# A copy moved from ScalarE to GpSimd, and channel factors moved from SBUF to PSUM, in a kernel of four line scans and a dynamic-kernel convolution block

## The reference, cut to what matters

```python
def step(prev, cur):
    new = cur + jax.nn.relu(_row_conv(prev, K))     # 9 taps, 64 -> 64 channels
    return (new, new)
```

```python
pooled = x.mean((2, 3)); hdn = _ln(pooled @ w_fc1.T, ln1_w, ln1_b); dyn = hdn @ w_fc2.T
out = depthwise_conv(x, dyn.reshape(b * c, 1, 5, 5), pad=2)
out = layer norm of out over the channels
out = gelu(einsum('bchw,oc->bohw', out, w_expand))            # 64 -> 256 channels
gx = sqrt(sum(out ** 2, axis=(2, 3)));  nx = gx / (gx.mean(1) + EPS)
out = g * (out * nx) + bt + out                                # the "response"
return einsum('bohw,co->bchw', out, w_shrink) + x
```

## Time and profile before

| | us |
|---|---|
| median of 3 runs | 860.77 (859.72 to 861.04) |
| profiled execution, its own time | 859.75 |
| its span | 857.8 |
| TensorE busy in the span | 783.1 (91%) |
| VectorE busy | 620.9 (72%) |
| GpSimd busy | 454.5 (53%) |
| ScalarE busy | 407.9 (48%) |

### The profile page before, as it was taken

How to read it: one execution, slowest core, us unless ns; L and a number is a source line. 1 busy time by engine, 2 the same in 40 slices (tenths; PEclk the granted TensorE clock), 3 DMA queues, 4 the chain that set the end, 5 groups by cost and what they waited for, 6 DMA issues and landing times. The chain is left out here.

```text
span 857.8 us, 15635 instructions
## 1 busy us (share of the span) xinstructions
PE 783.1 (91%) x5399; PEld 637.1 (74%) x5399; DVE 620.9 (72%) x1130; ACT 407.9 (48%) x495; POOL 454.5 (53%) x444
## 2 busy tenths in 40 slices
PE   5999999999999999999999957677899998999796
PEld 5999998999999999999999956444444444444232
DVE  4666666666666666658888867888889898998944
ACT  5690004767770000000000014389999999999771
POOL 2333333333333333338888845698686787877520
PEclk9999999999999999999999978799999999999999
DMA  6760000000000000000000010221234343333314
GB/s 145 166 157 0 0 0 2 0 0 0 0 1 1 0 0 0 0 1 1 0 0 0 0 49 0 64 64 51 55 93 100 87 99 76 77 79 86 84 34 99
DMA packets 61572, 35.81 MB, mean 42 GB/s; under 512 B 41504, under 2 KB 59488, under 8 KB 61536
## 3 DMA queue, kind: packets, MB, share of 16 engines
q1 hardware_dynamic: 61536, 35.36, 17.2%
HBM read 17.85 MB, written 9.37 MB: 32 GB/s over the span
## 5 line engine op out<-in xcount | busy, mean ns | idle before, releaser
L481 PE MATMUL psum<-line_hi,taps_hi 128*128 128x256 f32 x1270 | 203.0, 292 | 11.7 <-DVE taps_lo L377 8.4
L495 PE MATMUL psum<-line_lo,taps_hi 128*128 128x256 f32 x1270 | 202.5, 291 | 0.9 <-DVE line_lo L430 0.8
L489 PE MATMUL psum<-line_hi,taps_lo 128*128 128x256 f32 x1270 | 202.3, 291 | 0.0
L430 DVE SCALAR_TENSOR_TENSOR line_lo<-psum,rest 128x256 fp32r<-128x256 f32 x254 | 108.1, 426 | 123.9 <-POOL rest L262 114.8
L481 PEld LDWEIGHTS psum<-line_hi,taps_hi 128*128 128x128 f32 x1270 | 177.1, 192 | 12.9 <-issue 9.2
L495 PEld LDWEIGHTS psum<-line_lo,taps_hi 128*128 128x128 f32 x1270 | 176.5, 191 | 2.0 <-DVE line_lo L430 1.8
L489 PEld LDWEIGHTS psum<-line_hi,taps_lo 128*128 128x128 f32 x1270 | 177.0, 191 | 0.0
L262 POOL TENSOR_TENSOR rest<-x,line_hi 128x256 f32<-128x256 f32 x127 | 82.9, 653 | 168.6 <-DVE line_hi L421 168.6
L314 ACT ACTIVATE by_h<-x (+1 forms) x128 | 85.7, 670 | 106.3 <-DVE x L410 104.7
L262 POOL TENSOR_TENSOR rest<-by_h,line_hi 128x256 f32<-128x256 f32 x127 | 91.6, 722 | 83.4 <-DVE line_hi L421 83.4
L753 POOL TENSOR_TENSOR part<-part,prod 128x960 f32<-128x960 f32 (+2 forms) x48 | 108.7, 2264 | 21.4 <-ACT prod L830 16.8
(11 more groups left out here) (135 smaller groups left out, 840.9 us busy)
## 6 DMA issues: line engine op xcount, KB each, us to landing
stage<-in_x_dram SPq DMA_DIRECT2D x32, 256.0 KB, 4.0
rstd_wide<-rstd_dram SPq DMA_DIRECT2D x30, 256.0 KB, 5.3
out_dram<-x SPq DMA_DIRECT2D x28, 256.0 KB, 5.4
crossed<-x SPq DMA_DIRECT2D x16, 256.0 KB, 3.5
crossed<-x SPq DMA_DIRECT2D x16, 240.0 KB, 3.5
out_dram<-x SPq DMA_DIRECT2D x8, 128.0 KB, 2.5
rstd_dram<-rstd SPq DMA_DIRECT2D x15, 64.0 KB, 1.5
fc_in<-in_L_conv_w_fc_dram SPq DMA_DIRECT2D x2, 100.0 KB
```

Source lines behind the costliest of these rows:

```text
L430: dve.scalar_tensor_tensor(out=line_lo[:, (slot + 1) % SLOTS, :, part], in0=as_lines(line_ps[slot][:, 0:LINE]), scalar=0.0, in1=as_lines(r ...
L481: mm = pe.matmul(line_ps[slot][:, 0:LINE], taps_hi[:, s, d, :], line_hi[:, slot, :, d:d + WP], start=(d == 0), stop=(d == OFFSETS - 1))
L489: pe.matmul(line_ps[slot][:, 0:LINE], taps_lo[:, s, d, :], line_hi[:, slot, :, d:d + WP], start=False, stop=False, skip_group_check=True)
L495: mm = pe.matmul(line_ps[slot][:, 0:LINE], taps_hi[:, s, d, :], line_lo[:, slot, :, d:d + WP], start=False, stop=(d == OFFSETS - 1), skip_ ...
```

## The change

`split_high` of the units 2 to 15 goes from ScalarE to GpSimd, as a `tensor_copy` just ahead of `split_low` of the same unit. The units 0 and 1 stay on ScalarE. For images 0 to 6 the `gamma` that L1012 reads, and the factors that L1015 writes and L1018 reads, lie in columns 260 to 261 and 264 to 265 of PSUM bank 7; `gamma` is copied there once at the start. The last image's response reads and writes SBUF as before.

```diff
+        gamma_ps = stat_ps[:, 2 * STAT_COLS + 4:2 * STAT_COLS + 4 + HALVES]
+        factor_ps = stat_ps[:, 2 * STAT_COLS + 8:2 * STAT_COLS + 8 + HALVES]
...
+            def split_high(u):                      # on GpSimd
+                pool.wait_ge(conv_done, 2 * (u - 1))
+                pool.tensor_copy(x_hi[:, u % 2, :, 2:2 + W],
+                                 x[:, u // 2, ROWS * (u % 2):ROWS * (u % 2 + 1), :]).then_inc(xhi_ready, 1)
+
             def split_low(u):
-                pool.wait_ge(conv_done, 2 * (u - 1))
                 pool.wait_ge(xhi_ready, u + 1)
...
                 if s + 2 < UNITS:
+                    split_high(s + 2)
                     split_low(s + 2)
...
-                if 2 <= s + 2 < UNITS:              # on ScalarE
-                    split_high(s + 2)
                 if w in range(UNITS):
                     square(w)
...
+                gamma, factor = (gamma_ps, factor_ps) if b < B - 1 else (kept["gamma"][:, :], resp[:, 5, :])
                 dve.scalar_tensor_tensor(out=resp[:, 4, :], in0=resp[:, 1, :], scalar=resp[:, 3, 0:1],
-                                         in1=kept["gamma"][:, :], op0=ALU.mult, op1=ALU.mult).then_inc(resp_step, 1)
+                                         in1=gamma, op0=ALU.mult, op1=ALU.mult).then_inc(resp_step, 1)
                 dve.wait_ge(resp_step, n + 3)
-                dve.tensor_scalar(resp[:, 5, :], resp[:, 4, :], 1.0, None, ALU.add).then_inc(resp_step, 1)
+                dve.tensor_scalar(factor, resp[:, 4, :], 1.0, None, ALU.add).then_inc(resp_step, 1)
                 dve.wait_ge(resp_step, n + 4)
                 shape = [P, HALVES, C]
                 dve.tensor_tensor(shrink_now[:, :, :], kept["shrink_t"][:, :, :],
-                                  resp[:, 5, :].rearrange("p (m a) -> p m a", a=1).to_broadcast(shape),
+                                  factor.rearrange("p (m a) -> p m a", a=1).to_broadcast(shape),
...
             dve.memset(crossed[0:C, 0, 0, :], 0.0)
+            dve.tensor_copy(gamma_ps, kept["gamma"][:, :])
```

More of the change, by code:

```diff
@@ L814, in split_high @@
             def split_high(u):
-                if u >= 2:
-                    act.wait_ge(conv_done, 2 * (u - 1))
                 act.activation(x_hi[:, u % 2, :, 2:2 + W], x[:, u // 2, ROWS * (u % 2):ROWS * (u % 2 + 1), :],
```

## The result

| kernel | median us (range, runs) | ratio to before [95%] | span of the profile | mean clock |
|---|---|---|---|---|
| before | 860.9 (859.72 to 861.48, 4) | 1 | 857.8 | 0.974 |
| changed | 853.86 (853.0 to 857.09, 4) | 0.9927 [0.9899, 0.9955] | 855.1 | 0.965 |
| changed, measured again | 852.87 (851.99 to 853.83, 5) | 0.9913 [0.9899, 0.9926] | 851.9 | 0.967 |

The change makes the kernel faster by 7.0 to 7.4 us, each median against its own runs of before (860.9, and 860.28 for the second); 9.25 were forecast. The first profile of the changed kernel is of the slowest of its four executions (857.09). Its second block starts at 505.11 us, that of the second profile at 502.31 and before's at 503.09, so 2.8 of the 3.2 us between the two profiles lie in the scans, which the change leaves alone.

What follows compares the result with a forecast made beforehand. VectorE bounds odd slots (15.81 of 16.06 us); in even slots no engine is full and a chain of waits through ScalarE, TensorE and VectorE decides. 7.0 + 1.9 + 0.35 = 9.25 takes the median from 860.77 to 851.5 us, range 850.2 to 854.2.

Steps and rivals of the forecast that it cites:

- Even slots 6 to 12: Four even slots of the second block: less ScalarE work and L1012 no longer waiting gain 1.73 + 3 x 1.76 = 7.0 us.
- one lies ahead of the response and the other in it: Even slots: reason why the gains of moving `x_hi` and freeing L1012 add, 0.69 + 0.99 = 1.68 us.
- The rival of the stall that stays: Something other than the second SBUF tensor holds L1012; four slots give 0.7 to 0.8 each, 855.5 us; chance 0.07.
- L1017 and L1023 in PSUM: Response (L1012, L1018 before): with one tensor in PSUM, as L957 has, neither is held by GpSimd; L1012 takes 0.22.
- Copy 1.04: GpSimd's new 128x1024 copy takes 1.04 us, estimated from smaller copies; bounds 0.61 and 2.01.
- the cover in the odd slots: GpSimd's 2.32 us idle before the addition in odd slots covers the copy, with 1.3 to spare.
- a copy of 2.01: Upper bound for GpSimd's copy: slot 3 would gain only 575.92 - 575.86, so the sum falls by 0.9.
- So the whole 0.95 between the starts of `x_hi` and of the squares is won, twice: 1.9: Slots 3 and 4: TensorE idles 2.55 us before the statistics, so moving `x_hi` off ScalarE gains 1.9 us.
- With `x_hi` gone the idle time is 1.6 and the fall may stay out… I count half, 0.35: TensorE's clock at slot 4's statistics: avoiding a fall that lost 0.69 counts half, gain 0.35; bounds 0 and 0.69.
- TensorE the bound: Rival: TensorE's list, ending 0.5 later in even slots, pushes each next odd slot; price 2.0, 853.5 us; chance 0.08.
- GpSimd the bound: Rival: a copy of 3.0 us costs five odd slots 0.68 each and slot 3 0.93; 856.8 us; chance 0.07.
- the slower side: Rival: a copy of 4.2 us in GpSimd's queue ahead of odd slots' additions makes it slower, 864.8 us; chance 0.04.

Runs made afterwards that it cites:

- the full-clock pair: Unread TensorE products, cut to the traced idle times, in the kernel before and in the changed kernel: 854.63 against 845.58 us.
- the kernel in which it does stay: Changed kernel with `x_hi` on GpSimd, but `gamma` and the channel factors left in SBUF: 862.25 us, ratio 1.0016 to before.
- one spare copy: Changed kernel with one extra 128x1024 GpSimd copy ahead of the real one in each slot that has one: 853.2 us, 0.9918.
- The kernel with the early `x_hi` on ScalarE: Changed kernel with `x_hi` of units 2 to 4 back on ScalarE: 854.66 us, 0.9935.
- two spare copies: Changed kernel with two extra 128x1024 GpSimd copies ahead of the real one in each slot that has one: 854.68 us, 0.9932.
- The generous pair: Unread TensorE products in generous counts, not cut to the idle times, in the kernel before and in the changed kernel: 857.16 against 849.6 us.

## Why the prediction was right or wrong

**Even slots 6 to 12: right.** 7.0 was forecast, the full-clock pair shows 7.12 for slots 6 to 14 (1.76 to 1.79 for each of the four). That slot 14 was a trial of both edits held to 0.01 us. The reason given for adding the parts, "one lies ahead of the response and the other in it", is wrong all the same, and only the observed slot saved the number: alone, `x_hi` makes the even slot 0.71 longer, and PSUM makes it 0.81 shorter (0.99 forecast). The rival of the stall that stays was priced at 855.5; the kernel in which it does stay took 862.25. It assumed one held instruction, and there were three, one behind the other.

**L1017 and L1023 in PSUM: right.** L957 was a sound witness: a call with one tensor in PSUM isn't held. L1020 was missed: as L1015 it had one tensor in, one out, both in SBUF, and no row of before showed it held, since GpSimd's second weight product had ended with L1012. I had not counted its move to PSUM as needed, and it is worth up to 1.03 us. The Trainium skill (SBUF — State Buffer, section "Who interferes with whom") says that an instruction of VectorE with two SBUF inputs contends with one of GpSimd that reads SBUF, and that `tensor_scalar` can contend as well, by a faster mode. The traces agree: L1020 takes 1.19 from SBUF to SBUF under GpSimd's work, and 0.16 with its output in PSUM. That a faster mode is the reason, no trace shows.

**Copy 1.04: right** (1.04 measured), and so was the cover in the odd slots: 1.3 to spare was forecast, 1.22 is there, and one spare copy costs nothing that the runs could tell. (The 575.92 in the price of a copy of 2.01 stands in no row. The squares of slot 3 start at 575.96, and the sum would fall by 0.85, not 0.9.)

**"So the whole 0.95 between the starts of `x_hi` and of the squares is won, twice: 1.9": too high.** At full clock slot 3 gains 1.28 and slot 4 1.07, but slot 2 loses 1.12 (16.11 to 17.23): 1.23 in all. There GpSimd had no idle time before its addition, which I had seen and checked only against the time when ScalarE is free, not against the length of the slot: `x_hi` in slots 0 to 2 stands in the prediction at nothing. The kernel with the early `x_hi` on ScalarE shows it: slot 2 is 16.12.

**"With `x_hi` gone the idle time is 1.6 and the fall may stay out… I count half, 0.35": this step failed.** Its bounds were 0 and 0.69 of gain. The idle time is 1.6, the fall at the statistics does stay out, and the clock falls further on instead, after an idle time of 2.20 ahead of the expansion, and stays down longer. The fall in slot 2 and those behind slot 14 had no term at all. They are there before the change too: slot 15 and the tail run at 0.91, which the page's slices, all 9 there, don't show.

By the table the falls cost the changed kernel 1.93 more in slots 2 to 5, 0.34 more in slots 6 to 14 and 1.75 more behind them, and 1.42 less ahead of slot 2: 2.6 us. But 0.78 of the gain ahead of slot 2 lies in the scans of these two executions (503.09 against 502.31 at the second block's start, 0.08 in the filled pair). Without the scans the profiles put the clock term at 3.3 us. They are of executions at the top and at the bottom of the clocks seen, so this is more than the typical cost. By the medians it is 9.05 - 7.4 = 1.6 to 9.05 - 7.0 = 2.0; by the means of all executions 8.6 - 6.7 = 1.9, with 0.9 to 3.0 as the 95% interval when the executions are drawn again at random. So the term was a cost of about 2 where a gain of 0.35 was put.

I asked of one fall whether it goes. The question for the whole block was where the clock falls once the idle times move. No loss stood in the term's bounds, so the range of 850.2 to 854.2 was built around a gain: scaled to the median of before, the two measurements of the change are 0.9927 x 860.77 = 854.5, above its upper end, and 0.9913 x 860.77 = 853.3, inside it.

Together: 7.12 + 1.23 + 0.18 - 0.03 = 8.5 at full clock by the spans, 9.05 by the medians, against 8.9 forecast without the clock term. Less 1.6 to 2.0 for the clock, the medians give the 7.0 to 7.4 measured. The whole 8.9 came nearer than its terms deserve: the early slots fell short by 0.67, and small gains elsewhere made up for part of it.

**TensorE the bound: not so** at the price named. It is busy for 19.62 of 20.12 in the even slots, and the odd ones don't grow. **GpSimd the bound, and the slower side:** the mechanism exists (two spare copies), its price isn't the one named: the even slot gives back 0.68 of 0.97.

**Open.** Why the falls behind slot 14 last longer in the changed kernel, where its work is the same to 0.03 us, isn't shown: only that filling the idle times removes them. Nor is it shown what makes one execution of a kernel run at a mean clock of 0.974 and another at 0.967. The generous pair, 7.56, had a clock that wasn't full on one side, so the clock's cost in the medians rests on the pair with cut counts alone. Why the kernel with early `x_hi` on ScalarE is slower than the changed one by its median stays open as well.

## What to carry to other kernels

If a small VectorE operation is held by GpSimd, look at the operands of every small one behind it: taking one out of the way, or shifting either list, hands the wait to the next. Here a slot of the same trace in which the edited work happened to be absent priced the edit better than the sum of parts did. Where TensorE idles for 1 to 3 us at a time, an edit off its path can cost or save us by its clock, here about 2; give that term both signs, look at the granted clock in windows of a few us, since a slice of the page at 9 can hold a fall, and measure the change with the idle times filled, cut to their lengths, before judging it. Compare the mean clock of the profiled execution with that of the others before a profile is taken as typical.

## What was not expected of the hardware

- Small VectorE instructions, two of 2 elements for each partition and one of 128, were held until GpSimd's running instruction ended, three in a row (0.45, 1.03 and 1.01 us over their free durations), also the one with a single SBUF tensor in and an SBUF tensor out (1.19 against 0.16).
- The clock's falls came at the same places in two traces of each kernel: 17.03 and 16.98 for slot 5 and 44.12 twice for the tail in the changed one, 42.14 and 42.22 for the tail in the one before. Yet the mean clock of a kernel's executions differs by up to 0.008. Removing 0.95 us of idle time ahead of the statistics didn't keep the clock up.
- Products that nobody reads gained 7.3 us in the changed kernel (852.87 to 845.59) and 5.7 in the one before (860.36 to 854.63) when cut to the idle times, and only 3.3 (852.87 to 849.6) when more of them were issued at the same places but one. With that place as well, the larger counts took 58.54 us for slot 15 and the tail, the cut ones 56.40, both at full clock.
